# Three last steps on VectorE cut into pieces in a graph and mixture-of-experts kernel: mish's end in four, the nodes' last subtraction in two

## The reference, cut to what matters

```python
def mish(x):
    return x * jnp.tanh(jax.nn.softplus(x))
x = mish(node_features @ W_dense.T + b_dense)
y = mish(edge_features @ W_edge.T + b_edge)          # 106250 x 256
msg = jax.nn.relu(x[src] + y)
agg = jax.ops.segment_sum(msg, dst, num_segments=node_features.shape[0])
rst = x + agg
return mish(rst @ W_out.T + b_out)
```

## Time and profile before

| what | value |
|---|---|
| median of 3 runs | 4284.08 us (4277.53 to 4288.81) |
| span of the profiled execution | 4272.1 us (the page gives no other time for it; the median is 12.0 us over it) |
| PE busy | 3514.0 us (82%) |
| POOL busy | 2823.4 us (66%) |
| DVE busy | 2295.0 us (54%) |
| ACT busy | 1939.7 us (45%) |
| mean granted TensorE clock | 0.848 |

### The profile page before, as it was taken

One profiled execution on the slowest core, in us unless ns is written; L12 is line 12 of the kernel. 1 busy time (PEld: TensorE's weight loads), 2 busy tenths in 40 slices (PEclk: granted clock), 3 DMA queues, 4 the chain that ended last, 5 costly groups with the idle time before them and its releaser, 6 DMA issues. The chain is left out here.

```text
span 4272.1 us, 68475 instructions
## 1 busy us (share of the span) xinstructions
PE 3514.0 (82%) x17723; PEld 3093.3 (72%) x17723; DVE 2295.0 (54%) x6976; ACT 1939.7 (45%) x3024; POOL 2823.4 (66%) x2732
## 2 busy tenths in 40 slices
PE   4777777777756899999999968888888888649999
PEld 4666666666645788888888867777777777538887
DVE  6566556556554445545445436666666666632222
ACT  4455555555541333333333445555555555423333
POOL 3677777777767777766676227777777777353444
PEclk7788788888776999999999987777777787559999
DMA  6455555555543222222222126666666666534443
GB/s 177 154 187 188 179 174 183 178 180 178 178 140 107 69 68 66 69 66 64 68 67 64 36 96 208 212 206 212 209 209 208 212 211 191 172 137 92 98 98 60
DMA packets 287817, 605.53 MB, mean 142 GB/s; under 512 B 61999, under 2 KB 163342, under 8 KB 287499
## 3 DMA queue, kind: packets, MB, share of 16 engines
q1 hardware_dynamic: 166267, 344.34, 25.0%
q0 software_dynamic: 114784, 245.67, 21.0%
q10 hardware_dynamic: 6576, 13.36, 0.9%
HBM read 460.33 MB, written 144.67 MB: 142 GB/s over the span
## 5 line engine op out<-in xcount | busy, mean ns | idle before, releaser
L1669 POOL DMA_INDIRECT y_node<-node_table,src_sb x832 | 847.6, 1019 | 379.2 <-issue 378.9
L509 POOL DMA_INDIRECT conv_gath<-support_table,src_sb x832 | 878.4, 1056 | 284.3 <-issue 259.9
L1110 POOL DMA_INDIRECT x_gath<-hidden_table,src_sb x832 | 792.9, 953 | 353.6 <-issue 259.9
L664 PE MATMUL conv_pz<-conv_we,conv_edge 128*128 128x256 f32 x2240 | 643.1, 451 | 76.9 <-PEq L97 76.7
L1682 PE MATMUL y_pa<-y_hot,y_node 128*128 128x64 f32 x3328 | 523.6, 326 | 181.7 <-PEq L97 181.1
L1682 PEld LDWEIGHTS y_pa<-y_hot,y_node 128*128 128x128 f32 x3328 | 506.8, 240 | 214.7 <-issue 212.0
L664 PEld LDWEIGHTS conv_pz<-conv_we,conv_edge 128*128 128x128 f32 x2240 | 510.2, 234 | 170.2 <-issue 81.4
L655 PE MATMUL conv_ps<-conv_hot,conv_gath 128*128 128x64 f32 x1664 | 255.6, 305 | 213.5 <-DMA conv_gath<-support_table,src_sb 210.9
L655 PEld LDWEIGHTS conv_ps<-conv_hot,conv_gath 128*128 128x128 f32 x1664 | 242.5, 219 | 245.9 <-DMA conv_gath<-support_table,src_sb 238.5
L1734 ACT ACTIVATE y_node<-y_node 128x1024 f32<-128x1024 f32 x208 | 219.4, 1056 | 340.6 <-ACTq L97 340.1
L1692 PE MATMUL y_pz<-y_we,y_edge 128*128 128x256 f32 x1104 | 361.0, 499 | 13.0 <-PEq L97 13.0
(11 more groups left out here) (256 smaller groups left out, 5844.8 us busy)
## 6 DMA issues: line engine op xcount, KB each, us to landing
conv_edge<-in_edge_t SPq DMA_DIRECT2D x140, 512.0 KB
edge_mish_table<-conv_neg SPq DMA_DIRECT2D x140, 512.0 KB
y_neg<-edge_mish_table SPq DMA_DIRECT2D x139, 512.0 KB, 4.2
y_edge<-in_edge_t SPq DMA_DIRECT2D x69, 512.0 KB
e_rows<-expert_rows SPq DMA_DIRECT2D x56, 272.0 KB, 3.3
conv_gath<-support_table,src_sb POOLq DMA_INDIRECT x832
x_gath<-hidden_table,src_sb POOLq DMA_INDIRECT x832
y_node<-node_table,src_sb POOLq DMA_INDIRECT x832, 3.1
```

Source lines behind the costliest of these rows:

```text
L509: pool.indirect_dma_start(gath[g % SLOTS][:, j, :], None, table[:, :], bass.IndirectOffsetOnAxis(ap=c.src[:, col:col + 1], axis=0),).then_ ...
L664: last = pe.matmul(ps_z[r % 2][:, j, :], edge[r][:, m, j * P:(j + 1) * P], we[:, m, :], start=m == 0, stop=m == KD - 1)
L1110: pool.indirect_dma_start(gath[g % SLOTS][:, j, :], None, table[:, :], bass.IndirectOffsetOnAxis(ap=c.src[:, col:col + 1], axis=0),).then_ ...
L1669: pool.indirect_dma_start(node[g % SLOTS][:, j, :], None, c.t3[:, :], bass.IndirectOffsetOnAxis(ap=c.src[:, col:col + 1], axis=0),).then_i ...
```

## The change

Three instructions are cut along their middle dimension, and only the last piece of each carries the semaphore. L529 (140 times) and L1790 (69 times), 128x1024 each, become four of 128x256. L1829 (35 times), 90x512, becomes two of 90x256. Nothing is moved: the order on every engine is the same, and the other engines' programs are unchanged. As two lines more stand in each place, L1669 of before is L1671 afterwards, L529 becomes L530, L1790 becomes L1793, and L1829 becomes L1834.

```diff
             def mish_end(r):
                 take(dve, q_ready[r])
-                link(dve, nc.vector.scalar_tensor_tensor(neg[r][:], q[r][:], -1.0, neg[r][:], ALU.add, ALU.mult), neg_own)
+                for j in range(CG):
+                    last = nc.vector.scalar_tensor_tensor(neg[r][:, j, :], q[r][:, j, :], -1.0, neg[r][:, j, :], ALU.add, ALU.mult)
+                link(dve, last, neg_own)
                 dve.sem_inc(neg_ready[r], 1)
...
             def mish_end(r):
                 take(dve, q_ready[r])
-                link(dve, nc.vector.scalar_tensor_tensor(z[r][:], q[r][:], -1.0, z[r][:], ALU.add, ALU.mult), own)
+                for j in range(CG):
+                    last = nc.vector.scalar_tensor_tensor(z[r][:, j, :], q[r][:, j, :], -1.0, z[r][:, j, :], ALU.add, ALU.mult)
+                link(dve, last, own)
...
                 take(dve, xo_in[b], 16)
-                link(dve, nc.vector.tensor_tensor(x, x, now, ALU.subtract), own)
+                for s in range(2):
+                    last = nc.vector.tensor_tensor(x[:, s, :], x[:, s, :], now[:, s, :], ALU.subtract)
+                link(dve, last, own)
                 dve.sem_inc(xo_ready, 1)
```

## The result

The changed kernel takes 4219.08 us (median of 4 runs, 4210.91 to 4221.73) against 4280.81 for the kernel before in the same job: ratio 0.9855, 95% interval 0.9841 to 0.9868, or 61.7 us faster. Forecast were 4230 us, 53.7 less. The profiled execution took 4210.91 us, its span is 4209.1, 63.0 under that of before. All times here are medians of fast runs: one execution further down (L529 alone, in two pieces) took 5484.1 us at a granted clock of 0.545 and is left out.

A forecast was written before the change was run, and what follows sets the result against it. The prediction took POOL's indirect gathers to bound both the first aggregation and the edge stage. Its terms, -40.1 - 10.9 - 4.7 + 2 = -53.7 us, took 4284.1 to 4230 us, range 4205 to 4250 (4202 to 4262 with rival 1 and the bound).

The forecast's parts named there:

- The bound and the lock: Both stages: POOL's gathers set the length; gathers wait for DVE's L529, L1790 and L1829 to end, costing 85.5 us.
- L529, forecast -40.1: First aggregation: four pieces cut 95 gathers' waits from 53.9 us, gaining 44.1, less 4.0 for the longer tail.
- the sum: Both stages' terms: -40.1 - 10.9 - 4.7 + 2 = -53.7 us, keeping every request at its old place.
- L1790, forecast -10.9: Edge stage: in four pieces, 50 requests and 19 in the longer tail wait 14.1 us instead of 25.0.
- L1829, forecast -4.7: Edge stage: in two pieces, 17 requests wait 0.11 us instead of 0.39, 6.6 us becoming 1.9.
- DVE's added time, forecast at 2 us under 474 us of free time: Both stages: 46 us more DVE work hides beside POOL's gathers; 2 us charged for openings and tails.
- Re-locking: Rival 1: requests lock elsewhere in DVE's sequence, losing half the gain or more; 4257 us, chance 0.17.
- No gain: Rival 2: the 0.81 us offset is coincidence, or another bound (PE, transfers) takes the gain; 4286 us, chance 0.08.
- The pieces hold together: Rival 3: pieces block a gather from first to last, so requests wait to 1.43 us; 4324 us, chance 0.05.

The follow-up runs named there:

- the second execution: The kernel before, unchanged, profiled once more to see how much its edge-stage gathers vary: one run, 4275.8 us.

## Why the prediction was right, and where it was not

**The bound and the lock: right.** In both stages a microsecond off the gathers came off the stage: 45.8 and 44.0 us, 26.1 and 26.1. In the edge stage that is the bound forecast; in the aggregation it held only as far as this change went, as the fourth point says. That L529 and L1790 held gathers up because of their second SBUF input is shown by the kernel in which a one-input instruction of the same length holds nobody up; behind the lines that stay, gathers still wait: the minimum (last section), L1804 (156 gathers, 17.0 us) and the one-hots (60, 3.5 us), all before. (878.4 + 259.9 us of the prediction counts 9.1 us of issue ahead of the first gather; without them 878.4 + 250.8 + 24.4 = 1153.6, the whole stage.) The Trainium skill (SBUF — State Buffer, "Who interferes with whom") says that a second SBUF input contends with GpSimd's reads, and the traces agree in so far as two-input instructions hold these gathers (95 and 53.9 us behind L529), without showing that it is a read. What it infers of descriptor generation, that tensor_tensor leaves it alone, does not hold for these indirect gathers: 17 waited 6.6 us behind L1829.

**L529, forecast -40.1: right, with some luck.** What remains behind its pieces is 14.1 us; the sum had 9.8 + 4.0 = 13.8. But it had 95 requests in the second piece and 41 in the tail, and there were 65 (all at 0.64 us, 7.6 us) and 69 (at 1.3, 6.3 us); the two differences cancel. The stage's gathers fell by 45.8 because the minimum's share changed too (35.2 to 28.1 us), which the sum had left out.

**L1790, forecast -10.9: too small by about half.** The places that the sum lists, taken to the next end, give 0.7 + 1.5 + 2.1 + 2.7 = 7.0 us, and the 19 in the tail at most 19 x 0.21 = 4.0: 11.0 us left at most, where the sum has 14.1, so by its own numbers the gain was 14.0 or more. Measured, 5.9 us were left of 25.0. The requests did keep their places (15 at 0.34 to 0.37 us, 5 at 0.46, 2 at 0.79, 1 at 0.84, 26 at 0.95 to 1.05, 20 in the tail); what the sum overlooked is that the 7 at 0.46 and 0.79, just behind a piece's end, were not held at all. And the 25.0 of before was the low end of 25.0 to 35.0; by itself the line gave 24 us (0.9943). L1829, forecast -4.7: 1.7 us left of 6.6, as forecast.

**DVE's added time, forecast at 2 us under 474 us of free time: wrong in its reason.** The busy time of the view of stages leaves out what DVE's sequencer does between instructions: 0.24 to 0.56 us at each signal, and over 4 us at the head of an iteration, where positions are read into registers (the view of L410, kernel after; 35 loads of 0.36 to 2.83 us, each followed by register work):

```profile
L410 DVEq TENSOR_LOAD <-conv_window x35: 363/1661/2826, 117.8 to 1219.7; - x35
```

Whether an idle stretch of DVE is a wait or such work can be told, because the trace also holds the sequencer's own instructions: where they lie end to end (about 0.09 us between two), DVE waits for nobody. In the kernel before, from 100 us after the first gather on, DVE stood still at a semaphore 37 times, 48.6 us in all (40.5 in the second execution): this, 1.5 us in each iteration of about 32 us, was its true slack, and not 474 us. In the kernel after it does so not once. The same add before and after:

```profile
486.65 0.22 DVE L537 TENSOR_TENSOR sums_table<-sums_table,conv_ps 128x64 f32 x1 [2.14 <-DVEq L97]
```

```profile
802.19 0.22 DVE L539 TENSOR_TENSOR sums_table<-sums_table,conv_ps 128x64 f32 x1 [0.52 <-DVEq L97]
```

Of the 2.14 us 1.62 are a wait; the 0.52 are hand-over alone. The gathers' gain (1.3 us per iteration) and DVE's added 0.84 us (4 x 0.21) used the slack up. So after the change this stage is bound by DVE's own program, from one end of the loop to the other, and a further microsecond off the gathers gives nothing there. The same holds for L529 alone, for both kernels with two pieces and the old order, and for all three with the minimum in pieces or from PSUM: no stop in any of them. Their times fit: the minimum in four adds 34 us to DVE's program (102.5 to 136.1); the one from PSUM adds 68 us of busy time and 14 of hand-overs (49.7 us ahead of L530, for 33.9 ahead of L525 and 2.1); by the ratios they lose 31 and 81 us on the change. Two pieces instead of four take off 0.13 x 140 = 18 us, and the ratio gives 15. That the 8.5 us lost in the tail are POOL running its full six groups ahead of DVE fits this, but no run tests it.

**The sum.** -53.7 forecast, -61.7 measured: the edge stage gave about 10 us more, the aggregation with its tail 5 us less than its term. That the total is within 8 us is thus in part two errors of opposite sign.

**The rivals.** Re-locking is real: the one-hots' new place moved the requests (873.1 us of gathers), but the change itself did not cause it. "No gain" is out, though its second bound exists: it is DVE's program, and it came just behind the gain. "The pieces hold together" was wrong for the change, where all 134 gathers that waited behind L530 got through at the end that was next due, but half right as a possibility: 31 gathers in one experiment, 35 in another, 34 in a third and 12 with the minimum in four waited for the last piece, past an end.

## What to carry to other kernels

Where GpSimd issues indirect transfers and is the bound, compare the mean of an issue with its median; here the difference, 93.0 us in the aggregation, was what VectorE's two-input and quick one-input instructions on SBUF cost it. A gather that waited ended a fixed time behind the instruction that held it (0.815 us here), which names the culprit line by line. Cut that instruction so that a piece ends where the requests fall, with as few pieces as will do, and look at what runs just ahead of the pieces. Count VectorE's free time from where it really stands still at a semaphore, with the sequencer's instructions in view, not from its busy share: here the next bound was 1.5 us per iteration away.

## What was not expected of the hardware

- A gather has two places where it can be held. A two-SBUF-input instruction holds the early one (it ends 0.815 us behind the instruction, 95 times in the aggregation of before). The quick minimum, one SBUF input, holds a late one as well: 72 gathers of before, 21.1 us, that start near the end of L523 end 0.12 us behind L525's end. With the minimum from PSUM both kinds are gone. With it in four pieces the late kind is gone, and the early one is down to 9.5 us.
- An instruction of 1210 ns with one SBUF input, the reduction, holds nothing at all, and neither does one from PSUM with one SBUF input.
- A request in the first moments of an instruction is not held: 16 gathers of before ask 0.12 to 0.13 us into L1790 and none is late. The same goes for a request just behind a piece's end, though the next piece has been running for about 0.12 us: 7 behind ends of L1790's pieces and 15 with L529 in two (at 0.73, the end at 0.69).
- The end of a piece lets a waiting gather through in some places and not in others, and it isn't the request's place that decides: with the minimum in four and the one-hots later, requests at 0.81 us and 20 at 0.93 to 0.95 waited to the last end, while 31 at 0.73 in the same kernel, and two at 0.93 with the minimum in four alone, got through at the next. What sorts them is what ran just ahead of the pieces. Where L529's pieces follow the row of one-hots, in the three kernels with the one-hots later, all 98 gathers that had an end to skip skipped it; where they follow the minimum, over eight kernels, 364 got through at the next end and 14 did not. Why the one-hots should do this, and what sets the 14 apart (all at 0.73 us, 12 of them in one kernel), is open; no run tests it.
